# Second edge stage of a graph kernel: the index copy and its waits move one gather forward on GpSimd's queue

## The chip, the cores and the metric

The kernel runs on one core of one Trainium2 chip. The metric is the device time of one execution in microseconds (us). The kernel before took 3897.82 us, the median of 3 timed runs (3890.13 to 3904.57).

## What is computed

The reference is two layers over a graph of 6,250 nodes with 256 channels and 106,250 edges sorted by destination. Each layer adds to the nodes a message passing step over the edges, a global linear attention, and a feed-forward block. The change lies in the message passing of the second layer, which is this, cut to what matters:

```python
h = silu(edge_scalars @ fc_w1 * c1) * SILU_NORM      # 8 numbers per edge
w = h @ fc_w2 * c2                                   # four weights of 64 per edge
xg0, xg1 = y0[edge_src], y1[edge_src]                # rows of the source node: the gather
mid0 = w_a * xg0 * ea0
mid1 = w_b * einsum("euc,ec->eu", xg1, ea1) * INV_SQRT3
mid2 = (w_c * xg0)[:, :, None] * ea1[:, None, :]
mid3 = (w_d * ea0)[:, :, None] * xg1
agg = segment_sum(concatenate([mid0, mid1, mid2, mid3], axis=1), edge_dst)
```

## The kernel before

The program is a row of stages: a front, the first edge stage, a middle, a feed-forward block, the second edge stage `edges1` (from L1905 on), and two closing stages. `edges1` is the one concerned.

**Tiling.** Edges are taken in 139 groups (`GROUPS1`) of 768. A group is six tiles of 128 edges (`T1` = 6), and the tiles are handled in three pairs. For a tile one indirect DMA on GpSimd's queue (L1984) fetches 128 rows of 256 floats from the table `tab1` in HBM, by the 128 numbers of one column of an index tile. A group has six such gathers, numbered 1 to 6 here and `j` = 0 to 5 in the code. They fill `rows`, which has five group buffers (`PER` = 5).

**Indices.** All indices lie in `srcI`. Inside the loop a gather reads them from the small tile `ix` of two buffers. One copy per group (L1982) puts the next group's six columns in the other buffer, which the group before the present one had used. The copy therefore may not be made before all gathers of that earlier group have read it; the waits for their landings see to that.

**Order on GpSimd's queue.** The order is written out by hand, in `step` below. `hold` (L124) is a wait on a semaphore followed by a no-operation; its waits appear as L127. Each of the six gathers of a group has its own semaphore, `s_row[0]` to `s_row[5]`, which a landing raises by 16. For a group inside the loop the order is: wait for the index copy (`s_ix`) and for a free buffer (`s_msg`, the message products of five groups back); waits for gathers 1 and 5 of the group before; gather 1; wait for gather 2 of the group before; gather 2; wait for gather 3 of the group before; gather 3; waits for gathers 4, 5 and 6 of the group before; wait for gather 2 of this group; the copy; gathers 4, 5 and 6.

**The other engines.** TensorE makes the edge weights (L2198, L2212), sums messages over destinations by products with one-hot matrices (L2226), turns the sums (L2236), and does the attention's products of the next stage between them (L2249, L2256). VectorE makes the one-hot matrices (L2134, L2142), the message products (L2156 and twice L2158 for each pair, which wait for that pair's two gathers) and adds the sums to the nodes' window (L2114). ScalarE applies the activation and copies. SyncE loads 36 KB of edge attributes per group on its own queue. `turns` unrolls ten groups per loop iteration.

Of the kernel before, what the change touches and what calls it, by code (L numbers as in the profile page):

```python
# [47 lines left out]
T1 = SUB * ST  # L48
GE1 = P * T1
FULL1 = E // GE1  # L50
GROUPS1 = FULL1 + 1
# [59 lines left out]
def turns(eng, body):  # L111


    m = 2 * PER
    for g in range(m):
        body(g, g, g, g, g // PER)
    with eng.Fori(1, LAST // m) as k:
        for r in range(m):
            body(k * m + r, r, m, LAST // m * m - 1, k * 2 + r // PER)
    for g in range(LAST // m * m, GROUPS1):  # L120
        body(g, g % m, g, g, g // PER)


def hold(eng, sem, value):  # L124

    eng.wait_ge(sem, value)
    eng.nop(nofuse=True)  # L127
# [1777 lines left out]
def edges1(env, z):  # L1905
# [3 lines left out]
    nc, a, sem, ident = (env[k] for k in ("nc", "a", "sem", "ident"))  # L1909
    srcI, baseI = env["srcI"], env["baseI"]  # L1910
# [3 lines left out]
    with ExitStack() as ctx:  # L1914
        sb = lambda n, s, d=F32: ctx.enter_context(nc.sbuf_tensor("e1_" + n, s, d))
        pb = lambda n, s: ctx.enter_context(nc.psum_tensor("e1_" + n, s, F32))
        ix = sb("ix", [P, 2, T1], I32)
# [24 lines left out]
        s_row = env["s_rows"][0:T1]  # L1942
        s_es = [sem(f"e1_es{i}") for i in range(PER)]
        s_ix, s_T, s_esT, s_F, s_h, s_W, s_msg, s_eq, s_oh, s_acc, s_us, s_flip, s_add = (
            sem("e1_" + n) for n in ("ix", "T", "esT", "F", "silu", "W", "msg", "equal", "oh", "acc", "copied", "flip",
                                     "added"))
# [16 lines left out]
        def one_pass():  # L1963
            with nc.Block() as block:
                @block.gpsimd
                def _(pool):
                    def step(g, r, lo, hi, c):
                        at = ix[:, r % 2, :] if lo >= 1 else srcI[:, 0:T1]
                        if lo >= 1:
                            pool.wait_ge(s_ix, g)  # L1970
                        if lo >= PER:
                            hold(pool, s_msg, PAIRS * (g - PER + 1))
                        for j in range(T1):
                            if lo >= 1:
                                for i in ((j,) if j < 3 else range(3, T1) if j == 3 else ()):
                                    hold(pool, s_row[i], 16 * g)
                            if j == 3:
                                hold(pool, s_row[1], 16 * (g + 1))
                            elif j == 0 and lo >= 1:
                                hold(pool, s_row[T1 - 2], 16 * g)  # L1980
                            if j == 3 and hi <= GROUPS1 - 2:
                                nc.gpsimd.tensor_copy(ix[:, (r + 1) % 2, :], srcI[:, bass.ds((g + 1) * T1, T1)])\  # L1982
                                  .then_inc(s_ix, 1)
                            nc.gpsimd.indirect_dma_start(  # L1984
                                out=rows[:, r % PER, j, :], out_offset=None, in_=env["tab1"],
                                in_offset=bass.IndirectOffsetOnAxis(ap=at[:, j:j + 1], axis=0))\
                              .then_inc(s_row[j], 16)
                    turns(pool, step)
# [1066 lines left out]
```

## Time and profile before

| what | value |
|---|---|
| timed runs | 3890.13, 3897.82, 3904.57 us |
| the profiled execution | 3894.28 us |
| its span from first to last instruction | 3892.4 us |
| TensorE busy | 3077.4 us (79%) |
| VectorE busy | 2265.2 us (58%) |
| ScalarE busy | 1431.5 us (37%) |
| GpSimd busy | 1897.1 us (49%) |
| mean granted clock of TensorE | 0.880 |
| gathers of the second edge stage | 834, of about 0.95 us each on GpSimd |
| index copies of the second edge stage | 138, of 0.19 us each |

The profile records one execution. A timeline row gives an instruction's start, its length, its engine and line, and in brackets the time that the engine stood idle before it with what ended that. For a gather the length is GpSimd's own work, not the transfer. "DMA ..." behind a row means that the landing of such a transfer ended the wait; "issue" means that nothing recorded ended it; "remote" that it was something the profile doesn't name. POOL is GpSimd, DVE is VectorE, PE is TensorE; a "q" behind an engine's name marks an instruction of its queue's sequencer, which isn't counted as busy.

### The profile page before, as it was taken

The page shows a single profiled execution, that of the slowest core. Times are in us where ns is not written, and L with a number is a line of the kernel's source. Part 1 is how long each engine was busy: PE and PEld are TensorE (multiplying, and loading weights), DVE is VectorE, ACT ScalarE, POOL GpSimd, SP SyncE. Part 2 cuts the span into 40 slices and gives each one's busy share as a digit, 9 for nine tenths or more (in the row PEclk, how much of TensorE's full clock was granted, in tenths as well). Part 3 has the DMA queues.
Part 4 walks back from the last instruction along what each step waited for, and adds up shares of the span by engine and source line. Part 5 has one row for each costly group of instructions (what it writes and reads, how often), then busy time and mean ns, then how long its engine had stood idle before and what let it go on. Part 6 is the DMA issues. An engine that isn't in the chain of part 4 may idle for free. (4 is left out here: it accounts for less than half of the span.)

```text
span 3892.4 us, 80642 instructions
## 1 busy us (share of the span) xinstructions
PE 3077.4 (79%) x22728; PEld 2325.2 (60%) x22728; DVE 2265.2 (58%) x6165; ACT 1431.5 (37%) x4367; POOL 1897.1 (49%) x2266
## 2 busy tenths in 40 slices
PE   6477777777777768879997887888888888888499
PEld 4366666665666656658885544555554554557488
DVE  5455555555555556757665655666666666666712
ACT  5122222222222213732332544455454544416422
POOL 3556566656666652101112656656655566541154
PEclk9788788878888879989997989998999988889799
DMA  6433333333333334743322333333333333325321
GB/s 196 124 85 89 85 88 85 88 83 88 88 88 87 88 97 123 199 112 90 89 82 86 90 88 90 91 90 89 90 89 87 90 90 90 94 79 160 116 53 48
DMA packets 239107, 375.93 MB, mean 97 GB/s; under 512 B 88190, under 2 KB 145606, under 8 KB 238762
## 3 DMA queue, kind: packets, MB, share of 16 engines
q0 software_dynamic: 89712, 230.26, 21.5%
q1 hardware_dynamic: 147482, 140.83, 12.9%
q10 hardware_dynamic: 1696, 2.62, 0.2%
q14 instruction: 164, 1.34, 0.1%
q8 instruction: 53, 0.87, 0.1%
HBM read 310.75 MB, written 62.84 MB: 96 GB/s over the span
## 5 line engine op out<-in xcount | busy, mean ns | idle before, releaser
L586 POOL DMA_INDIRECT e_rows<-tab,e_ix x830 | 794.0, 957 | 539.6 <-issue 253.3
L1984 POOL DMA_INDIRECT e_rows<-tab,e_ix x828 | 787.8, 951 | 432.4 <-issue 342.3
L981 PE MATMUL e_pU<-e_ohp,e_rows 128*128 128x128 f32 x3340 | 527.4, 320 | 74.7 <-issue 70.4
L981 PEld LDWEIGHTS e_pU<-e_ohp,e_rows 128*128 128x128 f32 x3340 | 501.6, 235 | 85.6 <-issue 79.0
L2226 PE MATMUL e_pU<-e_msg,e_oh 128*32 128x128 f32 (+1 forms) x6672 | 425.4, 324 | 57.9 <-issue 47.4
L695 ACT CAST e_ohT<-e_pT 64x640 bf16<-64x640 f32 x167 | 114.6, 686 | 886.4 <-remote 472.1
L2156 DVE TENSOR_TENSOR e_msg<-e_pW,e_rows 128x256 f32<-128x256 f32 x417 | 176.6, 423 | 450.9 <-remote 250.7
L2158 DVE TENSOR_TENSOR e_msg<-e_pW,e_rows 128x384 f32<-128x384 f32 x834 | 422.2, 548 | 0.0
L2212 PE MATMUL e_pW<-e_w,e_hT 64*128 64x256 f32 x1668 | 332.6, 449 | 75.1 <-DVE e_oh L2142 23.5
L2226 PEld LDWEIGHTS e_pU<-e_msg,e_oh 128*32 128x32 f32 x6672 | 262.9, 117 | 208.5 <-issue 151.4
L962 PE MATMUL e_pT<-ident,e_oh 128*64 128x128 f32 x835 | 149.7, 319 | 206.1 <-DVE e_oh L487 134.8
L2212 PEld LDWEIGHTS e_pW<-e_w,e_hT 64*128 64x128 f32 x1668 | 150.7, 198 | 168.0 <-issue 80.7
L962 PEld LDWEIGHTS e_pT<-ident,e_oh 128*64 128x64 f32 x835 | 95.3, 127 | 257.2 <-issue 250.6
L832 DVE TENSOR_TENSOR e_ohp<-window,e_p 128x1280 f32<-128x1280 f32 x167 | 245.8, 1472 | 1.3 <-issue 1.2
L2042 ACT COPY e_us<-e_pU 96x512 f32<-96x512 f32 x139 | 80.9, 582 | 431.0 <-PE e_pU L2226 268.1
L2249 PE MATMUL e_pKV<-e_wkv,ffn_norm 128*125 128x512 f32 x400 | 226.4, 696 | 0.0
L1674 POOL TENSOR_TENSOR m_rn<-m_ve,m_mhalf 125x2 f32<-125x2 f32 x50 | 45.6, 913 | 336.4 <-DVE m_ve L148 336.4
L985 PE MATMUL e_pU<-e_oh,e_p 128*64 128x64 f32 x1670 | 150.8, 236 | 55.6 <-issue 55.3
L810 DVE TENSOR_REDUCE e_lg<-e_pE 128x20 f32<-128x60 f32 x167 | 36.1, 216 | 270.2 <-remote 228.1
L1847 PE MATMUL m_pH<-m_xnT,m_w 128*128 128x250 f32 x800 | 178.0, 381 | 6.8 <-DMA m_w<-in_L_ffn_W 4.4
L1860 PE MATMUL m_pO<-m_w,m_hT 128*125 128x256 f32 x800 | 176.7, 379 | 0.0
L985 PEld LDWEIGHTS e_pU<-e_oh,e_p 128*64 128x64 f32 x1670 | 122.4, 146 | 85.6 <-issue 69.8
(453 smaller groups left out, 5696.4 us busy)
## 6 DMA issues: line engine op xcount, KB each, us to landing
e_rows<-tab,e_ix POOLq DMA_INDIRECT x1658
xnT<-f_xnT SPq DMA_DIRECT2D x25, 250.0 KB, 3.1
e_xk<-xnT SPq DMA_DIRECT2D x25, 250.0 KB
xnT<-b_xT SPq DMA_DIRECT2D x25, 250.0 KB, 2.9
m_xnT<-xnT SPq DMA_DIRECT2D x25, 250.0 KB
xnT<-m_xT SPq DMA_DIRECT2D x25, 250.0 KB, 2.7
ffn_norm<-xnT SPq DMA_DIRECT2D x25, 250.0 KB
tab<-f_hrow SPq DMA_DIRECT2D x25, 227.5 KB
```

What stands on the lines that cost most here:

```text
L586: nc.gpsimd.indirect_dma_start(out=rows[:, s, j, :], out_offset=None, in_=env["tab0"], in_offset=bass.IndirectOffsetOnAxis(ap=at[:, j:j + ...
L832: nc.vector.tensor_tensor(out=ohp[:, s % 3, :, :, :], in0=eq.unsqueeze(2).broadcast_to([P, GT, H0, W]), in1=p[:, s % 3, :, 0:H0].unsqueeze ...
L962: last = nc.tensor.transpose(pT[0:W, P * j:P * (j + 1)], oh[:, s, j, :], ident[:, :])
L981: nc.tensor.matmul(pU[:, s % 2, 2 * W * k:2 * W * (k + 1)], rows[:, s, j, 128 * k:128 * k + 128], ohp[:, s % 3, j, 2 * k:2 * k + 2, :], st ...
L985: last = nc.tensor.matmul(pU[0:D0, s % 2, 4 * W:5 * W], p[:, s % 3, j, :], oh[:, s, j, :], start=False, stop=j == GT - 1, skip_group_check ...
L1847: last = nc.tensor.matmul(pH[:, f // 2, (f % 2) * CH:(f % 2 + 1) * CH], w1[:, j, k, 128 * c:128 * c + 128], xnT[:, s, k, :], start=k == 0, ...
L1860: last = nc.tensor.matmul(pO[:, t * C:(t + 1) * C], hT[:, s % 2, f, t * R:t * R + R], w2[:, f, :], start=f == 0, stop=f == NF - 1)
L1984: nc.gpsimd.indirect_dma_start(out=rows[:, r % PER, j, :], out_offset=None, in_=env["tab1"], in_offset=bass.IndirectOffsetOnAxis(ap=at[:, ...
L2158: last = nc.vector.tensor_tensor(out=m[:, j, 1:7, :].rearrange("p (b q) c -> p b q c", b=2), in0=wa[:, j, :, 1:2, :].broadcast_to([P, 2, 3 ...
L2212: last = nc.tensor.matmul(region(i)[:, n, :], hT[64 * n:64 * n + 64, r % 2, i, :], w2[64 * n:64 * n + 64, :], start=True, stop=True)
L2226: last = nc.tensor.matmul(u8[:, 0:8:2, :] if c == 0 else u8[:, 1:2 + 2 * c:2 * c, :], oh[:, r % 2, ST * i + j, c, :], m[:, 0:4, :] if c == ...
L2249: last = nc.tensor.matmul(pKV[0:R, :], xk[:, k, t * R:t * R + R], wkv[:, k, HID * b:HID * b + HID], start=k == 0, stop=k == 1)
```

## The change

In `step` of `edges1`, the copy of the next group's indices and the waits for gathers 3 to 6 of the group before stand in front of the third gather. Before, the wait for gather 3 stood there, and the waits for gathers 4 to 6 and the copy stood in front of the fourth. The wait for gather 2 of the present group stays in front of the fourth gather and has no copy behind it any more. In the first group, which has no waits on a group before, the copy moves in the same way; the last group has no copy.

```diff
                         for j in range(T1):
-                            if lo >= 1:
-                                for i in ((j,) if j < 3 else range(3, T1) if j == 3 else ()):
+                            if j == 2:
+                                for i in range(2, T1) if lo >= 1 else ():
                                     hold(pool, s_row[i], 16 * g)
+                                if hi <= GROUPS1 - 2:
+                                    nc.gpsimd.tensor_copy(ix[:, (r + 1) % 2, :], srcI[:, bass.ds((g + 1) * T1, T1)])\
+                                      .then_inc(s_ix, 1)
+                            elif j < 2 and lo >= 1:
+                                hold(pool, s_row[j], 16 * g)
                             if j == 3:
                                 hold(pool, s_row[1], 16 * (g + 1))
                             elif j == 0 and lo >= 1:
                                 hold(pool, s_row[T1 - 2], 16 * g)
-                            if j == 3 and hi <= GROUPS1 - 2:
-                                nc.gpsimd.tensor_copy(ix[:, (r + 1) % 2, :], srcI[:, bass.ds((g + 1) * T1, T1)])\
-                                  .then_inc(s_ix, 1)
```

## Rows read from the trace of the kernel before

**Rows 1.** The page's costliest groups: busy, mean ns, idle before and its releasers.

```profile
L2156 DVE TENSOR_TENSOR e_msg<-e_pW,e_rows 128x256 f32<-128x256 f32 x417 | 176.6, 423 | 450.9 <-remote 250.7
```

**Rows 2.** Source view, gathers and first products, from 2102 us to 2290, then 2701.

```profile
L1984 POOL DMA_INDIRECT e_rows<-tab,e_ix x103: 943/949/978, 2121.7 to 2288.8; - x103
L1984 POOL DMA_INDIRECT e_rows<-tab,src x6: 946/949/1052, 2108.4 to 2119.4; - x6
...
L2156 DVE TENSOR_TENSOR e_msg<-e_pW,e_rows x54: 414/425/426, 2116.2 to 2290.0; 128x256 f32<-128x256 f32 x54
...
L1984 POOL DMA_INDIRECT e_rows<-tab,e_ix x354: 943/949/978, 2121.7 to 2698.8; - x177
...
L2156 DVE TENSOR_TENSOR e_msg<-e_pW,e_rows x173: 414/425/426, 2116.2 to 2700.7; 128x256 f32<-128x256 f32 x173
```

**Rows 3.** Source view of L2156, 2102 to 2290 us: idle us before it, times, by releaser.

```profile
  remote: 26.5, 9
  DMA e_rows<-tab,e_ix: 22.0, 14
```

**Rows 4.** Source view: ns min/median/max, first and last start; stage, opening, after the opening.

```profile
L1982 POOL COPY e_ix<-src x138: 187/188/190, 2116.2 to 3468.2; 128x6 int32 x110, 128x6 int32<-128x6 int32 x28
...
L1982 POOL COPY e_ix<-src x18: 187/188/190, 2116.2 to 2283.4; 128x6 int32<-128x6 int32 x10, 128x6 int32 x8
...
L2142 DVE TENSOR_TENSOR e_oh<-e_pW,e_edges x120: 957/958/959, 2306.1 to 3499.6; 128x768 f32<-128x768 f32 x120
```

**Rows 5.** Windows view: length, busy PE, PEld, DVE, ACT, POOL, granted clock, DMA share, GB/s.

```profile
2590.00:2890.00 300.00, 257.21 (x2303) 152.16 (x2305) 185.53 (x453) 148.46 (x626) 180.22 (x214) 0.90 0.32 90
```

**Rows 6.** Timeline of TensorE, two groups in a row.

```profile
2715.18 1.29 PE L2226 MATMUL e_pU<-e_msg,e_oh 128*32 128x256 f32 x24
...
2724.36 2.36 PE L2226 MATMUL e_pU<-e_msg,e_oh 128*32 128x256 f32 x24
```

**Rows 7.** Timeline of GpSimd, one whole group and the next one's first gather.

```profile
2701.09 0.94 POOL L1984 DMA_INDIRECT e_rows<-tab,e_ix  x1 [1.33 <-issue]
2702.34 0.95 POOL L1984 DMA_INDIRECT e_rows<-tab,e_ix  x1 [0.31 <-issue]
2703.59 0.95 POOL L1984 DMA_INDIRECT e_rows<-tab,e_ix  x1 [0.30 <-issue]
2705.25 0.19 POOL L1982 COPY e_ix<-src 128x6 int32 x1 [0.71 <-DMA e_rows<-tab,e_ix]
2705.93 0.97 POOL L1984 DMA_INDIRECT e_rows<-tab,e_ix  x1 [0.49 <-issue]
2707.21 0.95 POOL L1984 DMA_INDIRECT e_rows<-tab,e_ix  x1 [0.30 <-issue]
2708.46 0.95 POOL L1984 DMA_INDIRECT e_rows<-tab,e_ix  x1 [0.31 <-issue]
2710.75 0.95 POOL L1984 DMA_INDIRECT e_rows<-tab,e_ix  x1 [1.34 <-issue]
```

**Rows 8.** Source view of GpSimd's waits (L127) in four narrow stretches: when each passed.

```profile
L127 POOLq EVENT_SEMAPHORE  x1: 17/17/17, 2705.1 to 2705.1; - x1
...
L127 POOLq EVENT_SEMAPHORE  x1: 17/17/17, 2710.0 to 2710.0; - x1
...
L127 POOLq EVENT_SEMAPHORE  x1: 17/17/17, 2711.6 to 2711.6; - x1
...
L127 POOLq EVENT_SEMAPHORE  x1: 17/17/17, 2116.1 to 2116.1; - x1
```

**Rows 9.** Timeline of GpSimd, the stage's second gather and its first copy.

```profile
2109.74 0.95 POOL L1984 DMA_INDIRECT e_rows<-tab,src  x1 [0.31 <-issue]
...
2116.23 0.19 POOL L1982 COPY e_ix<-src 128x6 int32<-128x6 int32 x1 [4.29 <-DMA e_rows<-tab,src]
```

**Rows 10.** Timeline of VectorE beside the group of rows 7.

```profile
2703.63 1.12 DVE L2114 TENSOR_TENSOR sum<-sum,e_pU 128x128 f32 x3
...
2705.05 0.37 DVE L2134 TENSOR_TENSOR e_pW<-e_pW,dst_rel 128x192 f32<-128x192 f32 x1
```

## The prediction

> **What bounds the kernel now.** I read the page by stage first. The second edge stage begins with its first gather at 2108.4 us [rows 2] and starts its last group's one-hot product at 3499.6 us [rows 4], so some 1,400 us of the 3892.4 us span are open to this change; the rest of the program is not touched. The page's chain of work that ended last names only lines of the stage after the edges and says nothing here, so this stage has to be read by itself.
>
> In the list of costly groups VectorE's message products (L2156) stand idle 450.9 us, most of it for "remote", which names nobody [rows 1]. Whether they wait for gathered rows must be counted instead. By 2290 us 109 gathers (18 groups of six) have been issued and 54 first-of-pair products (18 groups of three) have started: GpSimd is less than one group ahead. By 2701 us it is 360 gathers against 173 products, 60 groups against 57.7; the distance grows on average by the difference of the cadences below [rows 2]. So the stage has two parts. In the **opening** of about 18 groups the rows are used as they land, and 14 of 54 products wait for a DMA by name, 22.0 us in all, with 26.5 us more "remote" [rows 3]. **After it** the rows lie groups ahead (2.3 groups, 23 us, by the middle); the gather queue may run late by that much without being seen.
>
> The two cadences say the same. The index copies, one a group, run from 2116.2 to 3468.2 us: 1352.0 / 137 = 9.87 us. In the opening it is 167.2 / 17 = 9.84 us. The one-hot products, one a group on the computing side, run from 2306.1 to 3499.6 us after the opening: 1193.5 / 119 = 10.03 us [rows 4]. GpSimd would finish a group 0.16 us sooner than TensorE, VectorE and ScalarE together can use it. What slows these is TensorE: 257 us busy of 300 in the middle stretch at a granted clock of 0.90 [rows 5]. The same 24 matmuls take 1.29 us in one group and 2.36 us in the next [rows 6], the two levels of 2.4 and 1.2 GHz.
>
> **GpSimd's own cycle.** Group 60 of the timeline [rows 7], its first gather set to 0: gathers at 0, 1.25 and 2.50, copy at 4.16, gathers at 4.84, 6.12 and 7.37, next group at 9.66. Engine gaps between queued gathers are 0.30 us. Two are longer, and they are waits for landings, seen in the queue's own semaphore instructions [rows 8]. One at 2705.1 ends the wait for the group's second gather (which ended at 2703.29, so 1.8 us after its end). The copy starts 0.15 us later and the fourth gather 0.8 us later. One at 2710.0 ends the wait for the fifth gather of the group before (ended 2708.16, again 1.8 us), and the first gather starts 0.75 us later with no copy between.
>
> **The change part by part.** Removed in front of the fourth gather: the copy and the three waits for gathers 4 to 6 of the group before. Added in front of the third: the same four, once for each of 138 groups. Kept in front of the fourth: the wait for this group's second gather. No transfer is added, no other queue is passed; the order on GpSimd's queue is all that changes, and the third gather's DMA is what moves later.
>
> - *The waits.* The sixth gather of the group before ends 1.34 us before time 0; with 1.8 us to land it is in at 0.46. The queue reaches the first of these waits at about 0.9 (the entry at 2711.6, which is 0.9 behind the first gather's start of 2710.75) [rows 7, 8]. Cost nothing. What hides them is the execution of the first two gathers, to 2.20.
> - *The copy ahead of the third gather.* It starts at 2.20 + at most 0.30 and takes 0.19 [rows 4], then a gap of 0.30 (queued) to 0.49 (as before the fourth gather now). The third gather starts at 3.0 to 3.2 instead of 2.50 and ends at 3.9 to 4.1. Who waits for it: the fourth gather behind it on the engine, possible from 4.2 to 4.4; and VectorE's second pair, which needs the third and fourth gathers' rows and so still waits for the fourth.
> - *The fourth gather.* It still waits for the second gather's landing, at 2.20 + 1.8 = 4.0. Then it starts after 0.75 us, not 0.83: 4.75 against 4.84. The copy's 0.19 and its gap of 0.49 do not come off, as the queue prepared the gather while the copy ran. The trace has no fourth gather without a copy inside the loop, so I bound this: at least 0, at most 0.38 a group (0.19 + 0.49 less the 0.30 that a queued gather has anyway). I take 0.1, the difference of the two releases measured [rows 8], because both are the same step, a landing followed by a gather.
> - *The rest of the group* is shifted with the fourth gather, and the next group's first gather, which waits for the fifth's landing, with it: a cadence of about 9.75 instead of 9.85. What hides the third gather's delay of 0.5 to 0.7 us is this wait, of which 0.3 to 0.5 us remain. If that cover were gone, copy and gap would stand on the path in either order, at the same price as now.
> - *First group.* It waits for nothing before the copy; its third gather starts some 0.6 us later and the fourth still sits behind the second's slow first landing (4.29 us of idle before the copy) [rows 9]. Gain 0.1 at most.
>
> **The sum.** In the opening 17 groups x 0.1 = 1.7 us if the gathers paced all of it. Only the waits that name a DMA certainly do, so 1 to 2 us. After the opening 0: the computing side needs 10.03 us a group and GpSimd only gets further ahead, until its five buffers are full. From the stage's last message product to the end nothing waits for a gather. Against the profiled execution of 3894.28 us (span 3892.4) that is 3892.8. The three timed runs have a median of 3897.82, 3.5 us above it; I take the same 1.5 us off: 3896. The ends of the unknown are 0 and 17 x 0.38 = 6.5 us.
>
> **Rivals.**
>
> *A. The gathers pace more than I count, faster by over 0.5%* (19.5 us, about what a measurement of this kernel can tell from no change). If the "remote" waits were rows all through the stage, 0.38 x 138 = 52 us could go, to 3845; with 0.1 only 14 us, to 3884. Against it: rows groups ahead [rows 2] and a computing cadence that is longer than the gathers' [rows 4]. Chance 0.04.
>
> *B. The third gather stands behind the sixth's landing, slower.* The new wait costs nothing at first: it costs from the point where the sixth gather lands later than 3.5 us after its end (1.34, and the 2.2 from time 0 that are left when the third gather is to start at 3.0 and needs 0.83 from a release with a copy). In steady running it lands after 1.8 us; the stage's first gathers took 5.4 (2110.69 to 2116.1) [rows 8, 9]. With 5.4 in every group the third gather would start at about 4.9, the fourth at 6.2 instead of 4.84, and the cadence would be 11.2, above 10.03: 17 x 1.35 + 121 x 1.17 = 165 us, so 4063. Single late landings move the first gather by as much and would cost about 1 us each. Chance 0.02.
>
> *C. The copy collides with VectorE, slower.* At its new place, about 2.5, VectorE runs the three window sums, 1.12 us [rows 10]. Held until they end, the third gather starts at 4.1 to 4.3 and ends at 5.1, the fourth starts at 5.5: 0.65 a group over today, a cadence of 10.5, above 10.03 by 0.47. In every group that gives 17 x 0.65 + 121 x 0.47 = 68 us, 3966. All 138 copies took 187 to 190 ns [rows 4], though some stood beside VectorE work, as the one at 2705.25 beside L2134 [rows 7, 10]; so none was ever held. Chance 0.02. The Trainium skill, "GPSIMD Engine Reference", sections "Specifications" and "Key points", says that GpSimd shares its SBUF interfaces with VectorE and contends with VectorE instructions that have two SBUF inputs or use two ports. By that rule the collision would be real for such instructions; the sums read one operand in PSUM, and the trace shows no copy that was stretched.
>
> *D. It does nothing at all.* If the fourth gather starts as before, 3898. This is inside "the same".
>
> **How the numbers follow.** My forecast and D together 0.92, A 0.04, B and C 0.04. The 1.5 us is far under the scatter of the timed runs, 3890.13 to 3904.57 us. The range is that scatter, 7 us to either side, around 3889.8 to 3897.8 (the bounds of the sum off the median), with a little more above for single late landings: 3884 to 3906. The rivals beyond it hold some 0.08. Faster by over 0.5% 0.04, within 0.5% 0.92, slower 0.04.
>
> **What would show it.** In the profile after, the gaps before third gathers hold the copy; copies start some 2.5 us after a group's first gather; third gathers start at 3.0 to 3.2, fourth gathers at 4.7 to 4.8; no DMA is named in front of the copy; copies come every 9.75 us in the opening; one-hot products after the opening still every 10.0 us; copies still last 188 ns. It is wrong if the copy's idle time stays near 0.8 us and names the sixth gather (B), if copies get longer (C), or if the one-hot cadence after the opening moves by more than 0.15 us (A).

## The result

The kernel with the change took 3924.48 us, the median of six runs (3914.09 to 3937.53), beside 3897.69 for the kernel before (3890.13 to 3908.25, six runs): a ratio of 1.0074, 95% interval 1.0051 to 1.0096. The forecast was 3896, range 3884 to 3906. The changed kernel is slower by 0.7%, and its time lies outside the range. The profiled execution took 3937.53 us, the slowest of the six, with a span of 3935.7 us, so the profiles of before and after lie 43 us apart where the medians lie 27 apart.

**GpSimd's cycle came out nearly as worked out.** This is GpSimd's timeline in the changed kernel (start, length, instruction; in brackets the idle time before it and what ended it). It answers to [rows 7].

```profile
2399.90 0.95 POOL L1986 DMA_INDIRECT e_rows<-tab,e_ix  x1 [1.25 <-issue]
2401.15 0.94 POOL L1986 DMA_INDIRECT e_rows<-tab,e_ix  x1 [0.30 <-issue]
2402.40 0.94 POOL L1986 DMA_INDIRECT e_rows<-tab,e_ix  x1 [0.30 <-issue]
2404.73 0.95 POOL L1986 DMA_INDIRECT e_rows<-tab,e_ix  x1 [1.39 <-issue]
2405.99 0.95 POOL L1986 DMA_INDIRECT e_rows<-tab,e_ix  x1 [0.30 <-issue]
2406.94 0.19 POOL L1978 COPY e_ix<-src 128x6 int32 x1
2407.30 0.97 POOL L1986 DMA_INDIRECT e_rows<-tab,e_ix  x1 [0.16 <-issue]
2409.61 0.95 POOL L1986 DMA_INDIRECT e_rows<-tab,e_ix  x1 [1.34 <-issue]
```

From the first gather at 2404.73: the second at 1.26, the copy at 2.21 directly behind it, the third at 2.57 (forecast 3.0 to 3.2), the fourth at 4.88 here. Over all groups the median from the second gather's end to the fourth's start fell from 2.71 to 2.58 us, and the median distance of two groups' first gathers from 9.72 to 9.62 us. The copies are the only thing that changed length, from 188 to 196 ns.

**The opening gained, what follows lost more.** First the source view of the gathers and the first-of-pair products up to 2290 us, then up to 2701 us (as [rows 2]), then the index copies and the one-hot products after the opening (as [rows 4]); each row gives shortest/median/longest ns, then the first and the last start.

```profile
L1986 POOL DMA_INDIRECT e_rows<-tab,e_ix x103: 943/949/976, 2124.6 to 2289.3; - x103
...
L2158 DVE TENSOR_TENSOR e_msg<-e_pW,e_rows x53: 415/425/426, 2119.1 to 2288.9; 128x256 f32<-128x256 f32 x53
...
L1986 POOL DMA_INDIRECT e_rows<-tab,e_ix x359: 943/949/984, 2124.6 to 2700.6; - x180
...
L2158 DVE TENSOR_TENSOR e_msg<-e_pW,e_rows x170: 415/425/426, 2119.1 to 2699.1; 128x256 f32<-128x256 f32 x170
...
L1978 POOL COPY e_ix<-src x138: 188/196/208, 2113.2 to 3503.2; 128x6 int32 x110, 128x6 int32<-128x6 int32 x28
...
L2144 DVE TENSOR_TENSOR e_oh<-e_pW,e_edges x120: 957/958/960, 2303.5 to 3542.6; 128x768 f32<-128x768 f32 x120
```

Over the first 18 groups the message products came every 9.75 us (9.93 before), some 3 us in all, between the 0 and 6.5 us that the forecast took as its ends. After the opening the one-hot products come every (3542.6 - 2303.5) / 119 = 10.41 us, where it was 10.03. By 2701 us there are 365 gathers against 170 products, 61 groups against 57: the distance grows faster, because the computing side is slower, not only because GpSimd is quicker. From the first to the last product the stage took 1387.2 us before and 1427.2 now, 40 us more; the other stages differ by a few us.

**Where it shows.** The page's group of the first products (L2158), to be read against [rows 1], then the gathers (L1986):

```profile
L2158 DVE TENSOR_TENSOR e_msg<-e_pW,e_rows 128x256 f32<-128x256 f32 x417 | 176.7, 424 | 490.2 <-remote 311.8
...
L1986 POOL DMA_INDIRECT e_rows<-tab,e_ix x828 | 788.1, 952 | 578.9 <-issue 382.3
```

And the windows view of the stretch of [rows 5] (length, busy PE, PEld, DVE, ACT, POOL, granted clock, DMA share, GB/s):

```profile
2590.00:2890.00 300.00, 242.34 (x2217) 144.03 (x2213) 176.43 (x429) 143.08 (x614) 171.62 (x204) 0.91 0.30 86
```

TensorE is less busy (242 us of 300 where it was 257) at the same clock (0.91 and 0.90), so it isn't the clock. VectorE's products wait 61 us more for "remote", the word that the forecast had passed over. The profile of the changed kernel also shows a state that the one of the kernel before doesn't: from group 58 on the five row buffers are at times full. 32 first gathers wait over 1.9 us for VectorE's products, and all waits of gathers for them together are 120.5 us (15.2 before, none over 0.3 us).

### The profile page after: what moved, and what is told of

It is laid out like the page before. It is cut to its first block and busy times, and to the rows that moved or that the text cites. A ratio compares the mean times of both kernels' runs of the same rounds, so it can differ in the third digit from the quotient of the medians.

```text
span 3935.7 us, 80642 instructions
## 1 busy us (share of the span) xinstructions
PE 3087.5 (78%) x22728; PEld 2331.3 (59%) x22728; DVE 2266.2 (58%) x6165; ACT 1432.5 (36%) x4367; POOL 1898.7 (48%) x2266
## 5 line engine op out<-in xcount | busy, mean ns | idle before, releaser
L1986 POOL DMA_INDIRECT e_rows<-tab,e_ix x828 | 788.1, 952 | 578.9 <-issue 382.3
L2228 PE MATMUL e_pU<-e_msg,e_oh 128*32 128x128 f32 (+1 forms) x6672 | 438.3, 325 | 80.5 <-issue 63.0
L2158 DVE TENSOR_TENSOR e_msg<-e_pW,e_rows 128x256 f32<-128x256 f32 x417 | 176.7, 424 | 490.2 <-remote 311.8
L2214 PE MATMUL e_pW<-e_w,e_hT 64*128 64x256 f32 x1668 | 338.8, 456 | 94.0 <-DVE e_msg L2160 47.9
L2214 PEld LDWEIGHTS e_pW<-e_w,e_hT 64*128 64x128 f32 x1668 | 154.0, 201 | 189.4 <-issue 70.9
L2251 PE MATMUL e_pKV<-e_wkv,ffn_norm 128*125 128x512 f32 x400 | 212.8, 658 | 0.0
```

The source lines that it names most:

```text
L1986: nc.gpsimd.indirect_dma_start(out=rows[:, r % PER, j, :], out_offset=None, in_=env["tab1"], in_offset=bass.IndirectOffsetOnAxis(ap=at[:, ...
L2214: last = nc.tensor.matmul(region(i)[:, n, :], hT[64 * n:64 * n + 64, r % 2, i, :], w2[64 * n:64 * n + 64, :], start=True, stop=True)
L2228: last = nc.tensor.matmul(u8[:, 0:8:2, :] if c == 0 else u8[:, 1:2 + 2 * c:2 * c, :], oh[:, r % 2, ST * i + j, c, :], m[:, 0:4, :] if c == ...
L2251: last = nc.tensor.matmul(pKV[0:R, :], xk[:, k, t * R:t * R + R], wkv[:, k, HID * b:HID * b + HID], start=k == 0, stop=k == 1)
```

## What "remote" is

The trace also records when each semaphore was raised. VectorE's first product of a pair waits for its two gathers and for the semaphore that TensorE's weight products (L2212, after the change L2214) raise. "Remote" stands where no recorded end of an instruction lies near the raise. These timelines are of the kernel **before**, TensorE and then VectorE, beside the second half of the group of [rows 7].

```profile
2707.42 0.70 PE L2212 MATMUL e_pW<-e_w,e_hT 64*128 64x256 f32 x4
2708.06 1.06 PE L2226 MATMUL e_pU<-e_msg,e_oh 128*32 128x256 f32 x16
2709.50 0.28 PE L2226 MATMUL e_pU<-e_msg,e_oh 128*32 128x128 f32 x1 [0.38 <-issue]
2710.23 0.50 PE L2226 MATMUL e_pU<-e_msg,e_oh 128*32 128x128 f32 x7 [0.45 <-issue]
```

```profile
2706.43 0.42 DVE L2156 TENSOR_TENSOR e_msg<-e_pW,e_rows 128x256 f32<-128x256 f32 x1
2706.77 1.01 DVE L2158 TENSOR_TENSOR e_msg<-e_pW,e_rows 128x384 f32<-128x384 f32 x2
2710.39 0.42 DVE L2156 TENSOR_TENSOR e_msg<-e_pW,e_rows 128x256 f32<-128x256 f32 x1 [2.61 <-remote]
```

GpSimd's rows for the same time stand in [rows 7]: the fifth gather starts at 2707.21, the sixth runs from 2708.46 to 2709.41. The weight product is over at 2708.12 by its record, and VectorE has the rows, groups ahead. It starts at 2710.39 all the same, 0.98 us after the end of the *sixth gather*. TensorE's own sums stall for nothing named until about the same time.

It is no single case. In the kernel before, 90 of 417 products have such a wait. 87 of them end behind the third (41) or the sixth (46) gather of a group, a median of 0.97 us after its end (10th to 90th percentile 0.89 to 1.08); those are the gathers that close an unbroken run of three. The other 3 end while the third gather runs, 0.7 us after the second. In the changed kernel it is 116 of 124, 0.97 us behind, and 7 of the other 8 end 0.7 us after the fifth or second gather, while the next one runs. From the records of the semaphore, counted from the start of the last recorded weight product, for groups 18 to 118:

```
kernel              raised late (over 1.5 us)   time beyond 0.8 us, sum   these 100 groups took
before              84 of 272                   167 us                    1015.9 us
e11_split_copy      94 of 284                   174 us                    1020.5 us
e10_waits_only      94 of 276                   185 us                    1034.6 us
changed, e5         95 of 270                   164 us                    1022.9 us
changed, e9         111 of 279                  203 us                    1060.4 us
changed             113 of 290                  214 us                    1058.3 us
e6_after_no_pacing  91 of 284                   209 us                    1126 us
e7_before_free      100 of 291                  398 us                    1325 us
e3_no_pacing        0 of 300                    0                         877 us
```

(Some of the 300 raises are missing in the records; the sums are over those that are there. Each line is one profiled execution. e5 to e7 ran on one other chip, e9 to e11 on a second, e3 on a third.) The 47 us more between the first and the sixth line go with 42 us more of time. The line of e6 doesn't fit as well: 42 us more of late raises, but 110 us more of time, so these raises are not all of the loss there. The computing side was never bound to 10.03 us a group: on the chip of e3 it keeps up with gathers that come every 8.76 us, with no late raise at all. Part of the 10.03 was time in which TensorE's results were seen late while GpSimd issued gathers. The Trainium skill, "Perfetto Trace Analysis", section "Tensor Engine Instruction (MATMUL, LD_WEIGHTS)", says that the end of a matmul in a profile is an estimate, and that its semaphore is raised only once PSUM has acknowledged the data. The trace agrees that the two come apart: in the kernel before the raise comes up to 4.06 us after the start of a product that lasts 0.45 us in the mean. Which step on the way to the raise is late, no run shows.

## The experiments

The theories of the start were WAITS and PLACE (the moved waits, or the new place of the copy and the third gather, cost something), PACE (the faster stream of gathers makes the computing side slower) and FULL (the buffers being full costs). Later ones were STALL and SUPPLY, forms of PACE in which TensorE idles for nothing named while gathers are issued, and for e12 BYTES (the traffic of the rows disturbs TensorE) against DESCRIPTORS (the making of the gathers does). The chips turned out to differ, so each ratio below is against the kernel before on the same chip, and its time is given:

```
chip   before, us   "remote" of the first products   runs
A      3552.79      none                             e1 to e4
B      3863.74      yes                              e5 to e8
C      3897.33      yes                              e9 to e12
D      3552.38      none                             e13 to e16
E      3549.30      none                             e17, e18
```

The record's own chip (3897.69) shows it.

**e1 and e10: the waits alone.** The waits for gathers 4 to 6 stand in front of the third gather as in the change, the copy in front of the fourth as before:

```diff
                             if j == 2:
                                 for i in range(2, T1) if lo >= 1 else ():
                                     hold(pool, s_row[i], 16 * g)
-                                if hi <= GROUPS1 - 2:
-                                    nc.gpsimd.tensor_copy(ix[:, (r + 1) % 2, :], ...)
...
+                            if j == 3 and hi <= GROUPS1 - 2:
+                                nc.gpsimd.tensor_copy(ix[:, (r + 1) % 2, :], ...)
```

> The waits for gathers 3 to 6 of the group before stand in front of the third gather, as in the changed kernel, but the copy stands in front of the fourth, as before. Measured so far: 3897.7 us before, 3924.5 us with the change; gathers went from a median 9.72 us a group to 9.62, and the computing side from 10.03 to some 10.4 after the opening. Theory PACE (a gather stream that runs faster than before gets in the way of the computing side): cadence 9.7, time 3898 +- 8. Theory PLACE (what hurts is the third gather and the copy at their new place in the group): 3898 +- 8 as well. Theory WAITS (the waits moved forward are what hurts): 3915 to 3930.

> The waits for gathers 3 to 6 of the group before moved forward, the copy left in its old place. Where the kernel before took 3553 us the ratio was 1.0007. Theory SUPPLY, as theory PLACE: 1.000 +- 0.002 in any condition, because neither the runs of gathers nor the cadence change. If the moved waits have a part in the loss: 1.003 or more where the kernel before takes over 3800 us.

Measured 1.0007 (0.9998 to 1.0017) on chip A, 0.9984 (0.9960 to 1.0008) on chip C. The waits cost nothing, as the prediction had it.

**e2 and e11: the place of the copy without its gain.** Half of the copy in front of the third gather, half in front of the fourth:

```diff
-                                    nc.gpsimd.tensor_copy(ix[:, (r + 1) % 2, :], srcI[:, bass.ds((g + 1) * T1, T1)])\
+                                    nc.gpsimd.tensor_copy(ix[:, (r + 1) % 2, 0:3], srcI[:, bass.ds((g + 1) * T1, 3)])\
...
+                                if hi <= GROUPS1 - 2:
+                                    nc.gpsimd.tensor_copy(ix[:, (r + 1) % 2, 3:6], srcI[:, bass.ds((g + 1) * T1 + 3, 3)])\
+                                      .then_inc(s_ix, 1)
```

> The changed kernel with its copy split in two halves of three columns: one in front of the third gather, one in front of the fourth, behind the wait for the second gather's landing. So the third gather stands where the change put it, and the fourth starts as late as before. Theory PACE: the cadence is back at 9.7 us and the time at 3898 +- 8. Theory PLACE: the time stays at 3915 to 3930 with the old cadence.

> Half of the copy in front of the third gather, half in front of the fourth, so that the third gather stands where the change put it and the cadence is the old 9.7 us. Where the kernel before took 3553 us the ratio was 1.0004. Where it takes over 3800 us: theory PACE (the cadence decides) 1.000 +- 0.002; theory PLACE (the third gather's place, hence the length of the pauses between runs of gathers, decides) 1.003 to 1.008.

Measured 1.0004 (0.9995 to 1.0014) and 1.0007 (0.9983 to 1.0031). The third gather stands where the change puts it (gap before it 0.16 us, as above), the fourth where it was before, and nothing is lost. PLACE is out. On chip C the changed kernel itself measured 1.0088 (e9, below); what it has and e11 has not is the fourth gather 0.1 us sooner, so the loss hangs on that.

**e3: the kernel before without the wait that spaces the groups.**

```diff
-                            elif j == 0 and lo >= 1:
-                                hold(pool, s_row[T1 - 2], 16 * g)
```

> The kernel before without the wait, in front of a group's first gather, for the fifth gather of the group before (it keeps all waits that protect the index tile). The queue gains up to 1.0 us a group: free cadence 8.7 to 8.9 us until the five buffers are full, then that of the computing side. Copy and third gather stand in their old places. Theory PACE: slower than the changed kernel or like it, 3920 to 3960. Theory PLACE: 3890 to 3900, with a gain of some us in the opening.

Measured 0.9589 (0.9573 to 0.9605) on chip A, groups every 8.76 us; neither theory's expectation allowed for that. There the gathers set the pace of all 139 groups, and taking 1 us a group off them takes 4% off the time. The page's group of the first products names a DMA, and no "remote" stands in its source view.

```profile
L2154 DVE TENSOR_TENSOR e_msg<-e_pW,e_rows 128x256 f32<-128x256 f32 x417 | 176.5, 423 | 285.3 <-DMA e_rows<-tab,e_ix 145.0
```

**e4, e14 and e17: less distance.** The kernel before, with the gathers held at three groups ahead:

```diff
-                        if lo >= PER:
-                            hold(pool, s_msg, PAIRS * (g - PER + 1))
+                        if lo >= 3:
+                            hold(pool, s_msg, PAIRS * (g - 2))
```

> The kernel before, but a group's first gather waits for the message products of three groups back instead of five, so that the gathers are tied to the products from early on, in a fixed phase to them. Theory FULL (time is lost once the gathers are held back by full buffers, as in the changed kernel from its 58th group on): 3920 to 3950, as nearly all groups after the opening are so tied. Theory PACE: 3895 to 3905, since the stream is not faster anywhere. Theory PLACE: 3895 to 3905.

> The kernel before, with the first gather of a group waiting for the products of the group three back and not five back. Two theories of the loss remain. FULL: the loss comes once the five buffers are full and the gathers are released by the products in a fixed phase (first at group 58 in the changed kernel, 32 such groups, never in the kernel before). Here that would be so from group 20 or so on, so FULL expects 1.005 or more, up to 1.03 if every tied group costs what the groups 58 to 90 of the changed kernel did (10.56 for 10.05 us). PACE: the loss comes with the rate of the gathers, 9.62 for 9.72 us a group, in an unbroken run over many groups; here the gathers are held back to the pace of the products (10.0 to 10.2 us a group), so PACE expects 0.99 to 1.001.

> The kernel before, with the first gather of a group waiting for the products of the group three back. On a chip whose TensorE shows unnamed idle time in the stage (kernel before at 3860 us or more): FULL (the loss comes from full buffers, the gathers released by the products in a fixed phase) expects 1.005 to 1.03; PACE (the loss comes from the gathers' rate) expects 0.99 to 1.001. On the other kind of chip (3553 us) 1.000 to 1.002, as in e14, where the gathers pace all groups and no buffer is ever full.

Measured 1.0010 (0.9999 to 1.0020), 1.0006 (0.9997 to 1.0016) and 1.0006 (0.9997 to 1.0015). All three ran on chips where the gathers are never more than about a group ahead of the products (9.9 us at most from a group's first gather to its first product), so no buffer is ever full and the runs say nothing of FULL. The traces of the chips with "remote" don't settle it either; us a group, by the first products:

```
                          groups 18 to 54   groups 54 to 118   first gathers held over 1.9 us
before                    10.35             10.05              none
changed                   10.62             10.56              32, from group 58
e5, changed (chip B)      10.38             10.14              15, from group 75
e9, changed (chip C)      10.50             10.66              28, from group 72
e10, waits only (chip C)  10.50             10.26              11, from group 74
e11, copy split (chip C)  10.48             10.05              4, from group 105
```

In the record's pair the changed kernel is slower before any gather is held, which speaks against FULL. On chip C it isn't: there the loss lies wholly in the groups 54 to 118, and the groups within three of a held one take 10.83 us, the others 10.13. In e10, with 11 held gathers and nothing lost, it is the other way round, 10.10 and 10.51. Held gathers can also be what follows from slow products, and not their cause. So FULL stays a rival for the 27 us.

**e5, e9 and e13: the changed kernel on three more chips.**

> The changed kernel itself, once more, beside the kernel before. In the last comparison the kernel before took 3552.8 us, not 3897.7, and the whole stage ran at the gathers' pace (9.7 to 9.8 us a group on both sides, lead 4 to 8 us throughout), with no TensorE idle time that nothing explains; in the profile of before there were 83 us of that, and the computing side paced from the 18th group on. Theory STALL (whoever paces depends on whether TensorE has such stalls; where it hasn't, the gathers pace all 139 groups): ratio 0.995 to 0.997, that is 0.1 us x 138 = 14 us faster; where it has, ratio 1.005 to 1.009. Theory PLACE (the third gather's new place costs as such): ratio 1.004 to 1.010 in either condition.

> The changed kernel once more. Known by now: where the kernel before takes some 3860 to 3900 us, TensorE idles 80 to 110 us of the stage for nothing named, and the change gave 1.0074 and 1.0031; where it takes some 3553 us it was not yet run. Theory SUPPLY (TensorE gets its next instructions late while a run of gathers is being worked off; the change packs the gathers more densely): 1.003 to 1.008 where the kernel before takes over 3800 us; 0.995 to 0.998 where it takes some 3553 us, as the gathers pace all groups there and each is 0.1 us sooner. Theory PLACE: 1.003 to 1.008 in both.

> The changed kernel again, as the yardstick for the three kernels run beside it on this chip. Where TensorE shows idle time for nothing named in the second edge stage (83 us before and 112 us after in the first pair of profiles), the ratio should be 1.003 to 1.009, as in the earlier runs of it (1.0031, 1.0074, 1.0088). On a chip whose TensorE shows none of it, and where the gathers pace all groups, it should be 0.995 to 0.999 (0.12 us on each of 139 groups is 17 us at the most).

Measured 1.0031 (1.0014 to 1.0048) on B, 1.0088 (1.0054 to 1.0121) on C, and 0.9947 (0.9928 to 0.9966) on D. The first is less than STALL expected there (1.005 to 1.009). On D the sign is the other one. The source view of its first products (idle us before them and times, by what ended it):

```profile
L2158 DVE TENSOR_TENSOR e_msg<-e_pW,e_rows x417: 411/425/426, 1802.0 to 3139.3; 128x256 f32<-128x256 f32 x139
its engine sat idle before it (us, times) until:
  DMA e_rows<-tab,e_ix: 257.5, 177
  PE e_pW L2214: 111.0, 81
```

There is no "remote". The gathers set the pace, every group gets its share, and 3552.38 - 3529.97 = 22 us over 139 groups is 0.16 us a group (19 us and 0.14 by the ratio): the 0.1 of the forecast, under-sized by a little, everywhere and not in 17 groups. Rival A was right there, with 19 to 22 us for the 14 that it gave to 0.1 a group.

**e6: the changed kernel without the wait that spaces the groups** (the edit of e3), on chip B.

> The changed kernel without the wait, in front of a group's first gather, for the fifth gather of the group before. In the kernel before, taking it away gave a cadence of 8.7 us and a ratio of 0.959 where the kernel before took 3552.8 us. Theory STALL: where gathers pace, cadence 8.5 to 8.6 us and ratio 0.955 to 0.96; where TensorE stalls, 1.00 to 1.02, as the faster stream only fills the buffers. Theory PLACE: ratio at least 0.005 above that of the kernel before with the same wait taken away.

Measured 1.0501 (1.0467 to 1.0535), far over the 1.00 to 1.02 of STALL. The same edit to the kernel before *gained* 4% on chip A (e3). Products come every 11.3 us, and remote waits are 372.4 us.

**e7 and e8: both spacing waits gone,** from the kernel before and from the changed one:

```diff
-                            if j == 3:
-                                hold(pool, s_row[1], 16 * (g + 1))
-                            elif j == 0 and lo >= 1:
-                                hold(pool, s_row[T1 - 2], 16 * g)
```

> The kernel before without both waits that only pace: the one for the fifth gather of the group before, and the one for the group's own second gather. Left are those that protect the index tile. The queue could issue a group in about 6 x 1.25 + 0.3 = 7.9 us. Theory STALL: where gathers paced, the computing side becomes the bound at some 8.4 to 8.7 us a group, ratio 0.945 to 0.958; where TensorE stalls, 1.00 to 1.02. Against it, a rival QUEUE: more gathers in flight at once land later (over 1.8 us after their end) or make the queue slow, cadence no better than 8.7.

> The changed kernel without both waits that only pace, so that the copy stands in front of the third gather and nothing is awaited in front of the fourth. Now the position of the copy has no landing to hide behind: copy and gap cost 0.35 to 0.5 us on the queue in either place, and the wait for the sixth gather of the group before comes at 0.5 to 1.5 us after the group's first gather's start. Theory STALL: same as the kernel before with both waits gone, within 0.3%. Theory PLACE: at least 0.5% slower than that.

Measured 1.1182 (1.1151 to 1.1213) and 1.1116 (1.1086 to 1.1146). Both are far over STALL's 1.00 to 1.02, and e8 is the faster by 0.6%, which neither theory had. Six gathers now make one run of 7.3 us. The source view of e7's first products, then its timelines of GpSimd, TensorE and VectorE:

```profile
L2152 DVE TENSOR_TENSOR e_msg<-e_pW,e_rows x417: 415/425/426, 2095.3 to 3921.5; 128x256 f32<-128x256 f32 x139
its engine sat idle before it (us, times) until:
  remote: 658.6, 133
```

```profile
2699.55 0.95 POOL L1980 DMA_INDIRECT e_rows<-tab,e_ix  x1 [5.46 <-DVE e_msg L2154]
2700.80 0.95 POOL L1980 DMA_INDIRECT e_rows<-tab,e_ix  x1 [0.30 <-issue]
2702.06 0.94 POOL L1980 DMA_INDIRECT e_rows<-tab,e_ix  x1 [0.30 <-issue]
2703.01 0.20 POOL L1978 COPY e_ix<-src 128x6 int32 x1
2703.37 0.97 POOL L1980 DMA_INDIRECT e_rows<-tab,e_ix  x1 [0.16 <-POOL e_ix L1978]
2704.64 0.95 POOL L1980 DMA_INDIRECT e_rows<-tab,e_ix  x1 [0.30 <-issue]
2705.90 0.94 POOL L1980 DMA_INDIRECT e_rows<-tab,e_ix  x1 [0.30 <-issue]
```

```profile
2701.48 0.70 PE L2208 MATMUL e_pW<-e_w,e_hT 64*128 64x256 f32 x4
2702.11 1.06 PE L2222 MATMUL e_pU<-e_msg,e_oh 128*32 128x256 f32 x14
2703.76 0.38 PE L2222 MATMUL e_pU<-e_msg,e_oh 128*32 128x128 f32 x2 [0.60 <-issue]
2705.20 0.38 PE L2222 MATMUL e_pU<-e_msg,e_oh 128*32 128x128 f32 x2 [1.05 <-issue]
2706.63 0.27 PE L2222 MATMUL e_pU<-e_msg,e_oh 128*32 128x128 f32 x1 [1.06 <-issue]
2707.35 0.27 PE L2222 MATMUL e_pU<-e_msg,e_oh 128*32 128x128 f32 x1 [0.45 <-issue]
2708.05 0.50 PE L2222 MATMUL e_pU<-e_msg,e_oh 128*32 128x128 f32 x4 [0.43 <-issue]
```

```profile
2708.15 0.42 DVE L2152 TENSOR_TENSOR e_msg<-e_pW,e_rows 128x256 f32<-128x256 f32 x1 [5.73 <-remote]
```

The weight product ends by its record at 2702.18. VectorE gets it at 2708.15, 1.31 us after the run's last gather (2706.84). Of 133 such waits 126 end behind the sixth gather, a median of 1.35 us after its end; the median wait of all 133 is 4.99 us (2.80 in the kernel before). With a run of twice the length the product waits 1.8 times as long. TensorE drips one or two matmuls at a time meanwhile. The granted clock is lower too, 0.80 in the stage (0.91 in the kernel before on the record's chip); how much of the 12% is the clock's was not taken apart.

Full buffers are not needed for this. In e6 and e7 the first held gather is that of group 10, but the products of groups 0 to 5 already come every 16.3 and 18.1 us, where the kernel before has 9.8. From group 10 on the gathers are held and come no faster than the products, so what differs there is how they are bunched, not their rate.

**e12: e7 with a quarter of the bytes.** Each gather fetches 64 columns of a row, and the other 192 are left out:

```diff
-                                out=rows[:, r % PER, j, :], out_offset=None, in_=env["tab1"],
+                                out=rows[:, r % PER, j, 0:64], out_offset=None, in_=env["tab1"].rearrange("n (q c) -> (n q) c", q=4),
```

> The kernel before without both pacing waits, with gathers that fetch only 64 of the 256 columns of a row (from wrong places in the table; columns 64 to 255 of the gathered rows are zeros set once, so that the values are not those of the reference). GpSimd's instructions are as many and as long, the gathers' bytes are a quarter. With full rows this gave 1.118, 316 us of unexplained TensorE idle time and a cadence of 13.3 us where the kernel before takes 3864 us. Theory BYTES (TensorE is disturbed by the traffic of the rows): the ratio drops to 1.00 or below there, the idle time to under 100 us. Theory DESCRIPTORS (by the making and reading of the 128 descriptors of each gather): the ratio stays over 1.08, the idle time over 250 us. Where the kernel before takes 3553 us both expect 0.94 to 0.96.

Measured 1.1216 (1.1164 to 1.1267), no better than e7's 1.1182, though that is a ratio of chip B and this one of chip C; remote waits 688.5 us. Between 2200 and 3400 us the DMA engines move 22 GB/s where they moved 67 in e7. So it isn't the bytes of the transfers. What is left is the number of gathers, the descriptors that each needs, and what GpSimd does to issue them; no run tells these apart.

**e15, e16 and e18: a slower stream.** The kernel before with one more copy, or three, behind the index copy:

```diff
+                            if j == 3:
+                                if lo >= 1:
+                                    hold(pool, s_sp, 1 * g)
+                                nc.gpsimd.tensor_copy(spare[:, 0, :], srcI[:, bass.ds(g * T1, T1)]).then_inc(s_sp, 1)
```

> The kernel before with one copy more of six columns behind the copy of the indices, into a buffer that nobody reads: some 0.2 to 0.3 us more between the third and the fourth gather, so gathers every 9.95 to 10.05 us in place of 9.72 to 9.83. PACE (the computing side is slower where gathers come faster) expects the computing side to need less than its 10.05 us a group and the time to stay or fall, 0.990 to 1.002, on a chip whose TensorE shows the unnamed idle time. That the gathers' rate has no effect on the computing side (the record's prediction) expects 1.000 to 1.004, the opening's 0.2 us a group and no more. On a chip without that idle time the gathers pace all 139 groups: 1.008 to 1.011.

> The kernel before with three such copies: 0.6 to 0.9 us more a group, gathers every 10.4 to 10.6 us, which then pace the whole stage. The stage would be 139 groups of 10.5 us, 1460 us for 1387, so both theories expect a slower kernel, 1.015 to 1.022. What tells them apart is TensorE's idle time for nothing named in the stage: by PACE it falls from 83 us to 50 us or less, and the busy time of its matmuls falls too; by the other it stays at 75 to 90 us.

> The kernel before with one copy more of six columns behind the copy of the indices: about 0.2 us more between the third and the fourth gather of each group. On a chip whose TensorE shows unnamed idle time in the stage (3860 us or more): PACE, taken both ways, expects 0.990 to 1.002, the products of the groups behind the opening no slower and the idle time below that of the kernel before; that the gathers' rate has no effect expects 1.000 to 1.002. On the other kind of chip 1.004 to 1.006, as in e15.

Measured 1.0047 (1.0031 to 1.0064), 1.0126 (1.0110 to 1.0143) and 1.0051 (1.0037 to 1.0065), all on chips without remote waits. The first two are under what was expected (1.008 and 1.015 at least). They don't test whether a slower stream gives time back where results come late. They do price a copy in that place: 15 us / 139 = 0.11 us for one, 43 / 139 = 0.31 for three, 0.10 each; on chip E one costs 19 / 139 = 0.13. That is over half of its 0.19 us of work, and it bears out the 0.1 us that the sum had taken from two waits of one group.

## Why the prediction was wrong

- *The waits cost nothing:* right (e10, 0.9984).
- *The fourth gather 0.1 us sooner:* right on the chip of the record (0.12), and with e15 and e16 the price is known from outside. The third gather came sooner than forecast (2.56, not 3.0 to 3.2), since the queue had the copy ready behind the second gather and the third behind the copy. It changes nothing.
- *The opening gains 1 to 2 us:* right in kind, about 3 us.
- *B, the sixth gather's landing, and C, the collision with VectorE:* neither came. The copies lengthened by 8 ns.
- *The range:* its lower centre, 3889.8, is a slip. The median less 6.5 us is 3891.3; the range to 3906 would have missed 3924.48 either way.
- **The step that failed** is in the sum: "After the opening 0: the computing side needs 10.03 us a group and GpSimd only gets further ahead, until its five buffers are full." The 10.03 us was read as a need of TensorE, VectorE and ScalarE that the gathers can't touch. In it lay 250.7 us of waits of VectorE [rows 1], nearly all of which end just behind GpSimd's runs of gathers. The prediction saw the number, said that "remote" names nobody, set it aside once the rows were shown to be groups ahead, and then named TensorE as what slows the computing side, by its busy time and its clock. In the profile after the change the stage's clock is the same 0.91, the stage takes 40 us more instead of 0 (10.41 us a group after the opening), and remote waits are up 61 us. Changing the pace of the gathers moved what had been held fixed.
- *The sign that I set for being wrong* was met: the one-hot cadence moved by 0.38 us, over the 0.15. It was listed under A as a faster one; a slower one had no rival. B and C took the cost to lie on GpSimd's queue.

**What stays open.** Why 0.1 us a group raises the late ones from 84 of 272 to 113 of 290 on the record's chip and gives 111 of 279 on C, where e10 and e11 have 94, but only 95 of 270 on B, is not settled. The runs of gathers fill 6.93 of 9.72 us in the kernel before (2.50 + 0.95 and 7.37 + 0.95 - 4.84, [rows 7]) and about 7.0 of 9.62 after, 71% and 73%, too little for it by itself. A product that is released by the end of a run starts its next round in a fixed place beside the gathers; in e7 126 of 133 do. That the two cycles lock more often when their lengths are so is my guess. FULL on a chip with remote waits, and a slower stream there, weren't tried: e14 to e18 were meant for it and ran on the other kind of chip. No version was found that beats the kernel before on both kinds.

## What to carry to other kernels

A queue that runs ahead of its consumers isn't thereby free: before an edit to it is costed at nothing, take the waits that the profile doesn't name and lay their ends beside the instructions of every other engine, that queue's first. Timelines of TensorE, VectorE and GpSimd in one 4 us window of the kernel before would have shown the product start 0.98 us behind the sixth gather. And a gain of 0.1 us a group can have either sign on two chips of one type, so the time of the kernel before on the same chip has to be the yardstick, and a pacing wait that looks idle (e3 0.959, e6 1.050) may be what keeps another engine's results coming.

## What the runs showed of the hardware

- "Late" is over 1.2 us here, and the counts are of groups 18 to 118. While GpSimd issues indirect gathers in an unbroken run, a weight product of TensorE that is issued within the run is in many cases seen by VectorE only 0.97 us after the run's last gather (run of three, 3.45 us), or 1.35 us after it (run of six, 7.3 us). In the kernel before 45 of 62 raises were late where the product was issued within 1.25 us of the start of a run's second gather, and none of 55 where it was issued later than that after the start of the third.
- Which product it is matters in a way that I can't explain: those of the first pair, with a transpose behind them, were late in 4 of 79 cases, those of the second, with the sums behind them, in 58 of 96, those of the third, with the turning of the sums behind them, in 39 of 97.
- It goes with the chip, as far as these runs tell (each chip was used for one set of runs only): two chips and the record's show it, three others (3549 to 3553 us for the kernel before) in none of their profiles. The granted clock in the stage doesn't tell them apart, 0.90 to 0.92 in before, after, e5 and e9 to e11, 0.89 to 0.90 in e1, e14, e17 and e13. The first edge stage shows it as well. Its transposed matrices on ScalarE, in the source view of the kernel before and then of the changed kernel on chip D:

```profile
L695 ACT CAST e_ohT<-e_pT x167: 686/686/687, 113.3 to 1488.1; 64x640 bf16<-64x640 f32 x167
...
  remote: 529.2, 59
```

```profile
L695 ACT CAST e_ohT<-e_pT x167: 686/686/687, 114.1 to 1176.2; 64x640 bf16<-64x640 f32 x167
...
  PE e_pT L962: 641.2, 163
```

From its first gather to its last that stage takes 1373 us on the one and 1066 on the other, so 307 us of the 345 us between the two kinds of chip lies there.
- A copy of 0.19 us between a landing and the fourth gather costs 0.10 to 0.13 us (e15, e16, e18); queued behind a running gather it makes the way to the next gather 0.36 us where it is 0.30 without.
